# Four-layer graph network on one core: a sixth place for split tiles in columns 2 to 5, and the two halves of a finished pair's split set apart

## The reference, cut to what matters

```python
# x: (2708, 512) f32, adj: (2708, 2708) f32 (0.6% filled, and the diagonal)
for layer in (0, 1, 2):
    h = maximum(layernorm(x), 0)
    x = x + act(normalised(adj) @ h @ W)         # layer 1: h @ W.T + b, no relu
h = maximum(layernorm(x), 0)                     # layer 3
# attn = softmax-like over exp(-leaky_relu(s_left + s_right)) where adj != 0
x = x + sigmoid(gate_a * (attn @ (h @ W_sa)) + gate_b * (adj @ (h @ W_gcnb) + b_gcnb))
```

## Time and profile before

| | before |
|---|---|
| time, median of 3 runs | 1804.05 us (1803.03 to 1804.29) |
| the profiled execution: its time | 1801.34 us |
| the profiled execution: its span | 1799.5 us |
| PE busy | 1705.1 us (95% of the span) |
| DVE busy | 1112.1 us (62%) |
| ACT, POOL busy | 774.1 us, 613.4 us |
| columns 2 to 5 of layer 0 | 162 to 402 us of the span |
| first steps of column 3, 4, 5 and 6 | at 235.5, 311.3, 358.5 and 407.4 us |

### The profile page before, as it was taken

One profiled execution on the slowest core, in us unless ns is written; L12 is line 12 of the kernel. 1 busy time (PEld: TensorE's weight loads), 2 busy tenths in 40 slices (PEclk: granted clock), 3 DMA queues, 4 the chain that ended last, 5 costly groups with the idle time before them and its releaser, 6 DMA issues.

```text
span 1799.5 us, 31706 instructions
## 1 busy us (share of the span) xinstructions
PE 1705.1 (95%) x12862; PEld 1165.8 (65%) x12862; DVE 1112.1 (62%) x1957; ACT 774.1 (43%) x1178; POOL 613.4 (34%) x567
## 2 busy tenths in 40 slices
PE   3999899899999998899999999999999999999996
PEld 1444344657786887778887887888789544444454
DVE  5786997866668774633543443454641576877765
ACT  5675555554444343322322222210111568768654
POOL 0001654526656653520312121111200446545431
PEclk9999999999999999999999999999999999999998
DMA  9985688788787868885674889776545443544423
GB/s 393 361 319 159 239 291 312 258 317 287 281 290 266 299 229 305 292 324 196 213 244 150 270 273 353 247 241 232 204 130 187 133 117 98 157 126 120 147 81 125
DMA packets 185560, 417.08 MB, mean 232 GB/s; under 512 B 18341, under 2 KB 79137, under 8 KB 181681
## 3 DMA queue, kind: packets, MB, share of 16 engines
q1 hardware_dynamic: 151544, 337.14, 55.5%
q10 hardware_dynamic: 33868, 77.90, 11.5%
HBM read 303.80 MB, written 111.17 MB: 231 GB/s over the span
## 4 chain that ended last, share of the span: by engine, by line
PE 74%; DVE 12%; DMA 5%; ACT 5%; issue 2%; POOL 2%; SPq 0%; ACTq 0%; DVEq 0%; POOLq 0%
PE ps L1107 14%; PE ps L1152 12%; PE ps L1153 11%; PE ps L1154 11%; PE ps L1199 7%; PE ps L1200 7%; PE ps L1201 7%; DVE U L1452 4%; DMA U<-in_adjT 3%; ACT U L1781 1%; DVE stage L1435 1%; DVE CT L1491 1%; DMA U<-in_adj 1%; ACT U L1704 1%; PE ps L1167 1%
## 5 line engine op out<-in xcount | busy, mean ns | idle before, releaser
L1152 PE MATMUL ps<-U,HB 128*128 128x256 f16 (+2 forms) x2520 | 635.4, 260 | 10.2 <-DMA U<-Ad 4.2
L1153 PE MATMUL ps<-U,HB 128*128 128x256 f16 (+2 forms) x2520 | 635.2, 260 | 0.0
L1154 PE MATMUL ps<-U,HB 128*128 128x256 f16 (+2 forms) x2520 | 635.0, 260 | 0.0
L1199 PE MATMUL ps<-U,HB 128*128 128x512 f16 (+3 forms) x960 | 342.4, 359 | 30.0 <-DVE U L1452 21.2
L1200 PE MATMUL ps<-U,HB 128*128 128x512 f16 (+3 forms) x960 | 342.1, 359 | 0.0
L1201 PE MATMUL ps<-U,HB 128*128 128x512 f16 (+3 forms) x960 | 341.5, 358 | 0.0
L1452 DVE SCALAR_TENSOR_TENSOR U<-U,cS 128x512 f16<-128x512 f32 (+6 forms) x255 | 251.7, 1009 | 117.1 <-ACT U L1781 116.2
L1107 PE MATMUL ps<-W,OT 128*128 128x512 f16 (+1 forms) x1320 | 304.3, 385 | 14.7 <-DVE xr L1521 10.0
L1781 ACT ACTIVATE U<-U,cS 128x512 f16<-128x512 f32 (+6 forms) x255 | 198.8, 804 | 178.2 <-POOL U L1975 61.6
L1152 PEld LDWEIGHTS ps<-U,HB 128*128 128x128 f16 x2520 | 246.7, 98 | 40.3 <-DVE U L1452 4.6
L1153 PEld LDWEIGHTS ps<-U,HB 128*128 128x128 f16 x2520 | 246.9, 98 | 26.6 <-issue 0.3
(11 more groups left out here) (204 smaller groups left out, 1953.4 us busy)
## 6 DMA issues: line engine op xcount, KB each, us to landing
U<-Ad SPq DMA_DIRECT2D x83, 896.0 KB, 5.8
U<-in_adjT SPq DMA_DIRECT2D x289, 256.0 KB, 4.5
Ad<-U ACTq DMA_DIRECT2D x35, 896.0 KB, 4.7
xd<-xr SPq DMA_DIRECT2D x84, 256.0 KB, 5.4
xr<-xd SPq DMA_DIRECT2D x84, 256.0 KB, 5.3
U<-in_adj SPq DMA_DIRECT2D x14, 1354.0 KB, 8.6
U<-Ad SPq DMA_DIRECT2D x23, 707.0 KB, 5.4
HBd<-stage ACTq DMA_DIRECT2D x16, 896.0 KB, 9.6
```

The source lines that it names most:

```text
L1152: eng.matmul(o, h[0], hi, start=J == 0 and a == 0, stop=False)
L1153: eng.matmul(o, h[0], lo, start=False, stop=False)
L1154: last = eng.matmul(o, h[1], hi, start=False, stop=to in "acg" and J == 9 and a == 1)
L1199: eng.matmul(o, h[0], hi, start=j == 0, stop=False)
```

## The change

One more place for split tiles (NSP = 6) is laid on unit 13 and used in columns 2 to 5, where a split is now put five steps ahead of its use. Layer 3 (columns from 24 on) and columns 0 and 1 keep five places. In the pairs made ahead the second half is planned 14 us after the loads, not 12. `w_fetch(1)` and `w_max(1)` are planned one step earlier. PE's and POOL's programs are the same as before; DVE's and ACT's are in another order from the end of column 1 to the end of column 5, and SP's at two places. Line numbers behind line 157 are one higher in the changed kernel.

```diff
-NSP = 5
+NSP = 6
...
     if _g < GW:
-        _take(("raw", _g, _j), (_lane if _lane < NRAW else NSP + _lane) * 1024, 1024, _lane)
-        _take(("sp", _g, _j), (NRAW + _n % NSP) * 1024, 1024, _n % NSP)
+        _take(("raw", _g, _j), (_lane if _lane < NRAW else NSP - 1 + _lane) * 1024, 1024, _lane)
+        _q = (_n - 2 * (NT - 1)) % NSP if _g >= 2 else _n % (NSP - 1)
+        _take(("sp", _g, _j), (NRAW + _q if _q < NSP - 1 else NRAW + NEXTRA + _q) * 1024, 1024, _q)
...
-        _take(("sp", _g, _j), (NRAW + _n % NSP) * 1024, 1024, _n % NSP)
+        _take(("sp", _g, _j), (NRAW + _n % (NSP - 1)) * 1024, 1024, _n % (NSP - 1))
...
-        while split < len(splits) and near(splits[split], u, LA, 10.4 if splits[split][1] >= GE else 9.6):
+        while split < len(splits) and near(splits[split], u, LA + (2 <= splits[split][1] < GW), 10.4 if splits[split][1] >= GE else 9.6):
...
-    weights(1, 3, 14, 17, 20, 21, 23, 25, 29)
+    weights(1, 3, 13, 16, 20, 21, 23, 25, 29)
...
-                           (11, "split", g, j), (12, "split", g, j + 1), (17, "a_keep", g, j)):
+                           (11, "split", g, j), (14, "split", g, j + 1), (17, "a_keep", g, j)):
```

## The result

The changed kernel takes 1806.94 us in the median of 11 runs (1805.05 to 1810.42), the kernel before 1803.02 (1797.22 to 1804.29), measured beside it. The medians differ by **3.9 us, slower**, which is 0.2%. The ratio is 1.003 with a 95% interval of 1.0019 to 1.004; it is not the ratio of the two medians, and as a time it is 5.4 us (3.4 to 7.2). That the kernel is slower is clear of the noise; by how much is known to some 2 us. The profiled execution has a span of 1803.2 us, 3.7 more than before.

What follows compares the result with a forecast made beforehand. DVE's work and the loop from a pair's second half to the next loads were taken to bound the stretch. Terms -2.7 + 2.7 + 2.1 - 0.7 + 2.6 = +4.0 us on 1804.05 gave 1808.0 us, bounds 1803 to 1813.

Steps and rivals of the forecast that it cites:

- What bounds: Columns 2 to 5: bound twice, by DVE's work and by a loop where the second half lets the next loads go.
- A: Columns 2 and 3: sixth place gains 5.2 us, later second half costs 2.5; net -2.7 us, bounds -5.2 and +0.6.
- rival 2: DVE is the bound, order is nothing: gains and losses cancel, late load hidden, 1804 us within 2 us; chance 0.07.
- rival 4: The loop decides: second half 5.8 us later each time delays SP's loads, A becomes +0.6, about 1813 us; chance 0.21.
- B: Start of column 4: the fifth split stands ahead of evacuate(3)'s copies, so PE waits for them; +2.7 us.
- C: Column 4: w_hi(1) and w_lo(1) come later, delaying w_fetch(2) and raw loads behind it on SP; +2.1 us, upper bound 5.
- D: End of column 4: split of (4, 14) ahead of w_max(2), against pair work now there too; net -0.7 us, bounds -3 and +1.
- E: Column 6: load of (6, 2), issued 6.7 us later, shares DMA engines with awaited raw tiles; +2.6 us, bounds 0 and 4.
- C's: Sign in column 4: w_fetch(2) issued 2 us later against the first step of column 4.
- E's: Sign in column 6: sums of (6, 6) over 5 us behind its first step, with a wait of PE behind them.
- rival 3: The clock stays up: the wait at 271.67, shortened by 2.6 us, brings no 1.2 GHz, 5.4 us more return; 1792.2 us; chance 0.07.

Runs made afterwards that it cites:

- experiment 1: Changed kernel with the second half of a pair planned at 12 us again, sixth place kept: 1801.80 us, ratio 0.9991 to the kernel before.
- experiment 2: Kernel before, five places, with only the second half planned at 14 us instead of 12: 1804.94 us, ratio 1.0008.
- Experiment 11: Changed kernel with evacuate ahead of the fifth split and w_fetch(2) three steps later, second half still at 14 us: 1805.46 us, ratio 1.0021.
- experiment 6: Changed kernel with second half at 12 us, evacuate ahead of the fifth split and w_fetch(2) three steps later: 1799.27 us, ratio 0.998 to the kernel before.
- Experiment 4: Changed kernel with the store of a pair planned 19 us after its loads instead of 17: 1805.68 us, ratio 1.0012 to the kernel before.
- experiment 5: Changed kernel with second half at 12 us and evacuate ahead of the fifth split at column ends: 1801.37 us, ratio 0.9992 to the kernel before.
- experiment 9: Kernel before with only the weights' load w_fetch(2) moved three steps later: 1798.96 us, ratio 0.9981.
- experiment 3: Changed kernel with evacuate ahead of the fifth split at the ends of columns 1 to 4: 1806.93 us, ratio 1.0018 to the kernel before.
- experiment 7: Changed kernel with only the weights' load w_fetch(2) moved three steps later: 1802.92 us, ratio 1.0001 to the kernel before.
- experiment 8: Kernel before with only the load of kept pair (6, 2) issued late, behind step (5, 20): 1801.44 us, ratio 0.9999.
- experiment 10: Experiment 6's kernel with POOL's two bias adds of a finished pair planned 4 us later: 1801.40 us, ratio 0.9999 to the kernel before.

## Why the prediction was right, and where its steps were not

The forecast was 1808.0 us and slower; measured was 1806.94. The sum of +4.0 us met the +3.9, but by luck: its terms were wrong by more than the total.

**What bounds.** Right in kind: the stretch is bound by the loop through the second half, and nearly all of the loss goes with it. Experiments 1, 2 and 11 price the step from 12 to 14 at 5.1, 2.0 and 6.2 us.

**A, the sixth place and the later half**, is the term that failed, by two sizes. The later half was put at 2.5 us, "nearer the lower end", for the reason that a pair in store covers it; it is 5.1. Experiment 11 has nothing else against experiment 6, and there it is 6.2. That (8, 1) would end 5.8 us later was read rightly (242.40, now 248.93, of which 0.7 is the shift of the execution); the failing step is to count less than half of it, and only once, where (6, 4) before it was 8.4 us late. SP stands for 82.8 us instead of 61.8, and on its queue raw tiles and x of the running column stand behind the pair's loads (the chain above), which I had not named for this wait. ACT's store of the pair waits for the same second half and has splits behind it; it was in the kernel's description and in no term of the sum. Experiment 4 puts it at about 1.3 us. The place was put at -5.2 for two emptyings. In the profile it gives 3.9 us by (2, 18) and 6.3 by (3, 12) with nothing in its way (experiment 5), so the price of a tile was about right; that the gain stays was wrong. By (4, 1) 1.1 us of it are left, since the next waits for DVE grow, and the median of experiment 1 has 1.2. Experiments 6 and 9, with and without the place, are alike. Here rival 2 was right. Net, A was forecast at -2.7; the two experiments give 5.1 - 1.2 = +3.9. That this is the whole of the result is so by construction, since experiment 1 keeps everything else of the change: what B to E cost is in these two numbers, and is priced below by what taking each away gave. It is rival 4's mechanism, with a larger price than its +0.6 for A; its sum, 1813 us, was too high.

**B, evacuate.** Right as a mechanism, a split with its raw load in front of the copies; wrong in place and price. The wait of 3.08 us is at the start of column 3, where I had counted nothing; at column 4, where I had put +2.7, it is 0.7, since PE was late itself. Its sign, a wait of PE at the first step of column 4, did not come. Taken away it gives nothing that the medians show: 1806.93 against 1806.94 in experiment 3, 1801.37 against 1801.80 in experiment 5.

**C, the weights' tile.** The delay came as forecast, 2.6 us against the first step of column 4 where 2.1 was said, and a larger wait of PE behind it. But by the medians the change's share in it is nothing: the edit that takes it away gives both kernels the same 4 us. By the profiles it is 1.6 us, 6.2 less the 4.6 that lie between experiments 7 and 9 at (4, 18). Both are inside the noise of the four medians, so the +2.1 is not refuted, only not seen. What I read as a turn on SP's queue was, by the rows of experiment 7 (0.6 of 5.1 us), for the larger part the 1024 KB ahead of the tiles, and it was a cost of the kernel before, where I took the waits of 1.07 and 3.30 us as given.

**D** was -0.7. In the profile the way from (4, 13) to (4, 18) takes 13.9 us instead of 13.4, so it is about +0.5.

**E, the load of (6, 2).** +2.6 was wrong, it is 0 (experiment 8; in the changed kernel too, the sums of (6, 6) come 4.3 us behind the first step of column 6, where it was 4.1). I had priced the bytes at 2.8 us of all engines. Why they cost nothing I did not separate; the tiles that POOL awaited were issued behind this load in either order.

So the total of +4.0 against a measured +3.9 is no merit of the sum: A was 6.6 us too low, and B to E, forecast at +6.7 together, give between nothing and 2 us when each is looked at by itself. Two errors of the same size cancelled. The direction was right because I had let the later half and its neighbours weigh against the place at all. Of the signs, A's came (PE's waits for low parts between 162 and 300 us fell from 12.0 to 9.4 us, SP's grew), C's came, B's and E's did not.

**Open** is what comes back behind the change. Up to the first step of column 6 the profile of the changed kernel has lost 6.5 us, at column 12 it has lost 3.0. Experiments 2 and 7 have 3.1 and -0.1 of this. The waits there end with chains that start from a DMA (PE waits 7.1 us for the adds into x, where it was 10.0), so that a PE that comes later waits less; I did not test it.

**The clock.** The level near 1.2 GHz did not go away with shorter waits, it moved: 0.58 in 236 to 240 us behind the wait for the copy, 0.66 in 273 to 278 us behind a wait of 2.32 us, 0.50 in 336 to 340 us behind the wait of 4.20. In 300 to 360 us the mean fell from 0.97 to 0.91; with the weights' load moved it is 0.97 in the changed kernel (experiment 7) and 1.00 in the kernel before (experiment 9). So a part of what that edit gives comes back through the clock: by these means at most 0.06 x 60 = 3.6 us and 0.03 x 60 = 1.8 us, an estimate. The Trainium skill's rule (TensorE: Matmul & The Clock Gate, "Part 1: The HAM clock gate"), that idleness brings the throttled rate back, agrees with these three. But one wait of 2.71 us, at 213.22, has 1.00 behind it (212 to 222 us), where before 2.88 us at 212.65 had brought 0.59 in 212 to 216. So rival 3's hope, that a wait shorter by one tile leaves the clock up, held at (2, 18) and fell in column 3.

## What to carry to other kernels

A place more in a store is worth its tile only until the next engine that is short; look for what lets the loads go before the store is made larger. When an order is moved by a few microseconds, list who waits for the moved instruction on the other engines' queues (here SP's loads and ACT's store) and price each. Of a DMA issued ahead of others count its bytes, not only its turn on the queue: moving one load of 1 MB behind a pair and three small tiles made both kernels 4 us faster. And a stage moved by 2 us in a plan can move by 8 on the engine, when it falls behind an instruction that has to wait itself.

## What the runs showed of the hardware

Operations of DVE on 128 x 2 elements took 0.15 to 0.17 us when POOL was idle and up to 1.19 us in stretches in which POOL ran additions with two tensors in SBUF without a pause. In experiment 6 (DVE, then POOL):

```profile
335.09 1.19 DVE L1410 TENSOR_TENSOR SC<-RD,DS 128x2 f32<-128x2 f32 x1
336.31 1.19 DVE L1412 SCALAR_TENSOR_TENSOR NB<-mv,SC 128x2 f32<-128x2 f32 x1
...
335.00 2.48 POOL L2003 TENSOR_TENSOR xr<-xr,bias 128x512 f32<-128x512 f32 x2
```

Seven such operations in a row (the expectation of experiment 10 says eight) took 4.6 us in front of a split for which PE waited 3.80 us. In experiment 10, with POOL's adds moved by 1.7 us, they took 3.4 us. Not each operation in such a stretch is slow: of the seven in experiment 10 three took 0.15 to 0.16 us, a reciprocal with one input, and two that began in the 0.08 us between two of POOL's additions. The Trainium skill (SBUF — State Buffer, section "Who interferes with whom") says that a VectorE instruction with two SBUF inputs contends with a GpSimd instruction that reads SBUF, and that one blocks until the other is done; the length of 1.19 us, near the 1.24 us of one of the two adds (2.48 / 2), agrees.
